# Softmax of a feed-forward attention block: sixteen ScalarE exponentials with bias and row sums, in place of one exponential between three VectorE passes

## The reference, cut to what matters

```
gate_v = x Ws                      top 2 of 8 experts per head, sigmoid weights -> mix_v
v      = mix_v . (x Wv)            [B, 16 heads, 56, 64]
scores = (q * scale) k^T           [B, 16 heads, 56, 56]
probs  = softmax(scores)
attn   = probs v
gate_o = x Wd                      top 2 of 8 experts per head -> mask_o
x      = x + sum over heads of (mask_o attn) Wo
```

## Time and profile before

| what | value |
|---|---|
| median of 3 runs | 551.34 us (551.05 to 553.38) |
| the profiled execution, its own time | 552.02 us |
| its span, first to last instruction | 550.0 us |
| busy share PE / DVE / ACT / POOL | 80% / 85% / 53% / 26% |
| granted TensorE clock, mean | 0.965 |

### The profile page before, as it was taken

The page is one execution under the profiler, slowest core; times in us unless marked ns, Lnnn a source line. Parts: engine busy times, 40 slices in busy tenths (PEclk is TensorE's granted clock), DMA queues, the critical chain, the costliest instruction groups (busy, mean ns, idle before and its releaser), DMA issues.

```text
span 550.0 us, 25189 instructions
## 1 busy us (share of the span) xinstructions
PE 437.6 (80%) x10768; PEld 366.0 (67%) x10768; DVE 468.2 (85%) x850; ACT 293.3 (53%) x400; POOL 143.1 (26%) x125
## 2 busy tenths in 40 slices
PE   1466889889988998658887888788888888887864
PEld 0245777777777877547776776677676767676754
DVE  2987778887888895579999999999999999999962
ACT  1254756766675674425544554555555455545631
POOL 8262767775777685000000000000000000000000
PEclk9987999999999999678999999999999999999996
DMA  7814443454345300000000000000000000000000
GB/s 175 265 40 133 137 155 116 135 182 141 114 161 177 120 1 4 1 1 3 8 3 4 4 4 0 4 4 2 2 4 4 0 4 4 4 0 4 7 7 5
DMA packets 18124, 29.44 MB, mean 54 GB/s; under 512 B 2988, under 2 KB 13996, under 8 KB 18092
## 3 DMA queue, kind: packets, MB, share of 16 engines
q1 hardware_dynamic: 18092, 28.97, 16.9%
HBM read 28.05 MB, written 0.92 MB: 53 GB/s over the span
## 4 chain that ended last, share of the span: by engine, by line
DVE 43%; PE 33%; issue 14%; ACT 6%; DVEq 1%; DMA 1%; SPq 1%; POOL 1%; ACTq 0%; POOLq 0%
DVE ctxf_all L856 8%; PE ps L958 6%; PE ps L1201 5%; DVE ctxf_all L827 5%; DVE rs L844 3%; PE ps L989 3%; DVE ctxT L653 3%; DVE ah L874 2%; DVE attnf L866 2%; ACT ah L557 2%; PE ps L1004 2%; PE ps L1005 2%; PE ps L1006 2%; PE ps L1014 2%; PE ps L1126 1%
## 5 line engine op out<-in xcount | busy, mean ns | idle before, releaser
L369 POOL TENSOR_TENSOR nat<-ctxf_all,nat 128x640 f16<-128x640 f32 x32 | 70.6, 2223 | 50.1 <-ACT nat L442 50.1
L958 PE MATMUL ps<-ident,nat 128*128 128x128 f16 x768 | 60.9, 225 | 10.0 <-DVE ctxT L653 5.2
L442 ACT CAST nat<-ctxf_all 128x1536 f16<-128x1536 f32 x32 | 45.5, 1470 | 39.2 <-PE ps L1006 39.2
L856 DVE TENSOR_TENSOR ctxf_all<-mixp,diag_h 128x3584 f16<-128x3584 f16 x32 | 63.2, 2014 | 0.0
L958 PEld LDWEIGHTS ps<-ident,nat 128*128 128x128 f16 x768 | 46.2, 100 | 23.4 <-issue 13.0
L1098 PE MATMUL ps<-xn,mT 128*128 128x112 f16 x256 | 41.9, 218 | 11.2 <-DVE mixp L851 11.2
L375 POOL TENSOR_TENSOR p<-pf,p 128x672 f16<-128x672 f32 x32 | 46.1, 1460 | 12.8 <-ACT pf L455 12.8
L653 DVE COPY ctxT<-ps 128x1024 f16<-128x1024 f16 x64 | 42.7, 685 | 4.7 <-PE ps L958 4.7
L1201 PE MATMUL ps<-ctxf_all,ah 128*64 128x112 f16 x1024 | 29.6, 219 | 18.5 <-DVE ah L874 18.4
L447 ACT COPY ctxT<-ps 128x1024 f16<-128x1024 f16 x32 | 33.0, 1033 | 20.3 <-PE ps L958 20.3
L973 PE MATMUL ps<-qk_cur,ctxT 128*128 128x56 f16 x384 | 33.5, 188 | 12.6 <-DVE ctxT L653 10.7
(11 more groups left out here) (169 smaller groups left out, 1288.3 us busy)
## 6 DMA issues: line engine op xcount, KB each, us to landing
ctxf_all<-in_ctx_dram SPq DMA_DIRECT2D x32, 704.0 KB
ctxf_all<-in_ctx_dram SPq DMA_DIRECT2D x32, 46.0 KB
x_all<-in_x_dram SPq DMA_DIRECT2D x2, 448.0 KB
out_dram<-y_all SPq DMA_DIRECT2D x32, 28.0 KB
ctxf_all<-in_ctx_dram SPq DMA_DIRECT2D x32, 18.0 KB
fwq_nat<-in_L_ffn_Wq_dram SPq DMA_DIRECT2D x1, 512.0 KB, 9.2
fwk_nat<-in_L_ffn_Wk_dram SPq DMA_DIRECT2D x1, 512.0 KB, 9.6
fwv_nat<-in_L_ffn_Wv_dram SPq DMA_DIRECT2D x1, 256.0 KB, 5.8
```

The lines of the kernel that those rows point to most:

```text
L369: pool.tensor_tensor(nat[k][:, 1, 7 * C:], ctxf[k][:, 7 * C:], nat[k][:, 0, 7 * C:], ALU.subtract).then_inc(natlo2, 1)
L442: act.copy(nat[k][:, 0, :], ctxf[k][:, :]).then_inc(nathi, 1)
L856: last = dve.tensor_tensor(dv[:, part, :, :, :], mixp[:, part, :, :].unsqueeze(2).broadcast_to((P, 2 * NQ, HALF, H)), diag_h[:, :, :].unsq ...
L958: last = pe.transpose(ps[:, (3 * b + c) % 2, :].bitcast(F16)[:, P * (j % 8):P * (j % 8) + P], nat[k][:, j // TK, C * (j % TK):C * (j % TK) ...
```

## The change

The scores' z are evacuated with the factor -SCALE instead of SCALE, so that PSUM holds the scores with their sign turned. DVE takes the row minimum `smn` of those (one 128x896 pass as before), and ACT computes exp(-1 * psum + smn) in 16 instructions of 128x56, each with its column of `smn` as bias and with `accum_out`, which leaves the row's sum in `rs`. The subtraction, its tile `ssub`, and the sum on DVE are gone. The 16 exponentials come in two groups of eight, ahead of `aT` and behind it. On DVE the minimum moves ahead of the low part of `ah`. On ACT `xnT_evac` moves ahead of the high part of `ah`, and `gates_out` from behind the exponential to ahead of it; on PE the gates move from behind the output mix to ahead of it. The evacuation of `vT` covers the same elements in another order: it reads PSUM with a stride of 8 elements and writes runs of 56, where it read runs and wrote with a stride of 128 elements.

```diff
@@ -154,8 +154,7 @@
         dv = ctxf_all[:, 0:n_dv].bitcast(F16).rearrange("p (s k t h) -> p s k t h", s=2, k=NQ * 2, h=H)
         dm = ctxf_all[:, n_dv:n_dv + n_dm].bitcast(F16).rearrange("p (k r t j) -> p k r t j", k=NQ * HG, r=2, j=E // 2)
         pj = ctxf_all[:, n_dv + n_dm:n_dv + n_dm + n_pj].bitcast(F16).rearrange("p (s k d) -> p s k d", s=2, d=DH)
-        smx = sb("smx", [P, 2 * K16])
-        ssub = sb("ssub", [P, 2 * K16, S])
+        smn = sb("smn", [P, 2 * K16])
         e_sb = sb("e_sb", [P, K16, 2, SLOT])
         rs = sb("rs", [P, K16 * 2])
         rinv = sb("rinv", [P, K16 * 2])
@@ -239,9 +238,7 @@
         f_z2e = sem("f_z2e")
         f_s = sem("f_s")
         f_mx = sem("f_mx")
-        f_sub = sem("f_sub")
         f_e = sem("f_e")
-        f_rs = sem("f_rs")
         f_ri = sem("f_ri")
         f_top = sem("f_top")
         f_mo = sem("f_mo")
@@ -518,13 +515,25 @@
                 after(act, f_sg, i)
                 act.activation(th[:, :, :], g_sb[:, 0:16, :], ACT.Tanh, scale=0.5).then_inc(f_th, 1)
+            def exps(i, b):
+
+                if b == 0:
+                    after(act, f_mx, i + 1)
+                    after(act, f_et, i)
+                    after(act, f_ri, i)
+                for k in range(K16):
+                    last = act.activation(e_sb[:, k, b, 0:S], ps[:, b, S * k:S * k + S], ACT.Exp,
+                                          bias=smn[:, K16 * b + k:K16 * b + k + 1], scale=-1.0,
+                                          accum_out=rs[:, 2 * k + b:2 * k + b + 1])
+                last.then_inc(f_e, 1)
+
             def iteration(i, front=True, back=True, nxt=True):
                 if back:
                     after(act, f_vt, i)
                     after(act, f_vv, i - 1)
-                    act.mul(vT[:, :, :, 0:S].rearrange("p h b t -> p b t h"),
-                            ps[:, 6:8, 0:8 * S].rearrange("p b (t h) -> p b t h", h=8), 1.0 / (MIX_UP * PJ_UP)).then_inc(f_vte, 1)
+                    act.mul(vT[:, :, :, 0:S], ps[:, 6:8, 0:8 * S].rearrange("p b (t h) -> p h b t", h=8),
+                            1.0 / (MIX_UP * PJ_UP)).then_inc(f_vte, 1)
                 if front:
                     after(act, f_pj, i + 1)
@@ -533,7 +542,7 @@
                     act.copy(pj[:, 0, :, :], ps[:, 3, :].rearrange("p (q d) -> p q d", d=DH)).then_inc(f_pje, 1)
                     after(act, f_z1, i + 1)
                     after(act, f_s, i)
-                    act.mul(z[:, 0:8, :].rearrange("p (a k) n -> p a (k n)", a=2), ps[:, 0:2, 0:8 * S], SCALE).then_inc(f_z1e, 1)
+                    act.mul(z[:, 0:8, :].rearrange("p (a k) n -> p a (k n)", a=2), ps[:, 0:2, 0:8 * S], -SCALE).then_inc(f_z1e, 1)
                     after(act, f_tr, i + 1)
                     after(act, f_d, i)
@@ -547,7 +556,9 @@
                     after(act, f_z2, i + 1)
                     after(act, f_s, i)
-                    act.mul(z[:, 8:16, :].rearrange("p (a k) n -> p a (k n)", a=2), ps[:, 2:4, 0:8 * S], SCALE).then_inc(f_z2e, 1)
+                    act.mul(z[:, 8:16, :].rearrange("p (a k) n -> p a (k n)", a=2), ps[:, 2:4, 0:8 * S], -SCALE).then_inc(f_z2e, 1)
+                if nxt:
+                    xnT_evac(i + 1)
                 if back:
                     after(act, f_a, i - 1)
@@ -556,7 +567,9 @@
                         after(act, f_nrm, 2 * i - 1 + b)
                         act.copy(ah[:, k, 0, :], attnf[:, k, :]).then_inc(f_ahi, 1)
                 if nxt:
-                    xnT_evac(i + 1)
+                    gates_out(i + 1)
+                if front:
+                    exps(i, 0)
                 if back:
                     after(act, f_a, i)
@@ -564,14 +577,7 @@
                     act.copy(aT[:, :, :, 0:S],
                              ps[:, 4, 0:8 * S].rearrange("p (b t j) -> p j b t", b=2, j=E // 2)).then_inc(f_ae, 1)
                 if front:
-
-                    after(act, f_sub, i + 1)
-                    after(act, f_et, i)
-                    after(act, f_rs, i)
-                    act.activation(e_sb[:, :, :, 0:S].rearrange("p k b j -> p b k j"),
-                                   ssub[:, :, :].rearrange("p (b k) j -> p b k j", b=2), ACT.Exp).then_inc(f_e, 1)
-                if nxt:
-                    gates_out(i + 1)
+                    exps(i, 1)
                 if front:
                     after(act, f_et, i + 1)
@@ -840,9 +846,7 @@
                     normalise(i + 1)
                 if back:
-                    after(dve, f_e, i)
-                    dve.tensor_reduce(rs[:, :], e_sb[:, :, :, 0:S].rearrange("p k b j -> p (k b) j"), AX.X, ALU.add).then_inc(f_rs, 1)
-                    dve.wait_ge(f_rs, i)
+                    after(dve, f_e, 2 * i)
                     dve.reciprocal(rinv[:, :], rs[:, :]).then_inc(f_ri, 1)
                 if front:
@@ -866,22 +870,19 @@
                         dve.tensor_tensor(attnf[:, k, :], ps[:, 6 + b, :].rearrange("p (k d) -> p k d", d=DH),
                                           rinv[:, :].rearrange("p (k b) -> p b k", b=2)[:, b, :].unsqueeze(2).broadcast_to((P, K16, DH)),
                                           ALU.mult).then_inc(f_nrm, 1)
+                if front:
+
+                    after(dve, f_s, i + 1)
+                    after(dve, f_e, 2 * i)
+                    dve.tensor_reduce(smn[:, :], ps[:, 0:2, 0:8 * S].rearrange("p b (k j) -> p b k j", j=S), AX.X, ALU.min).then_inc(f_mx, 1)
+                if back:
+
                     after(dve, f_a, i - 1)
                     for b in range(2):
                         k = slice(K16 * b, K16 * b + K16)
                         dve.wait_ge(f_nrm, 2 * i - 1 + b)
                         dve.wait_ge(f_ahi, 2 * i - 1 + b)
                         dve.tensor_tensor(ah[:, k, 1, :], attnf[:, k, :], ah[:, k, 0, :], ALU.subtract).then_inc(f_alo, 1)
-                if front:
-
-                    after(dve, f_s, i + 1)
-                    dve.tensor_reduce(smx[:, :], ps[:, 0:2, 0:8 * S].rearrange("p b (k j) -> p b k j", j=S), AX.X, ALU.max).then_inc(f_mx, 1)
-                    dve.wait_ge(f_mx, i + 1)
-                    after(dve, f_e, i)
-                    dve.tensor_tensor(ssub[:, :, :].rearrange("p (b k) j -> p b k j", b=2),
-                                      ps[:, 0:2, 0:8 * S].rearrange("p b (k j) -> p b k j", j=S),
-                                      smx[:, :].rearrange("p (b k) -> p b k", b=2).unsqueeze(3).broadcast_to((P, 2, K16, S)),
-                                      ALU.subtract).then_inc(f_sub, 1)
                 if nxt:
                     low_tokens(i + 1)
                 if front:
@@ -1188,6 +1189,7 @@
                     last.then_inc(f_s, 1)
                 if nxt:
                     xn_turn(i + 1)
+                    gates(i + 1)
                 if back:
                     after(pe, f_dm, i)
@@ -1202,8 +1204,6 @@
                                                      dm[:, n, r, :, :].rearrange("p t j -> p (t j)"),
                                                      start=(hg + a == 0), stop=(hg == HG - 1 and a == 1))
                     last.then_inc(f_a, 1)
-                if nxt:
-                    gates(i + 1)
                 if back:
                     after(pe, f_ae, i)
                     if front:
@@ -1214,8 +1214,7 @@
                     last.then_inc(f_o, 1)
                 if front:
-                    after(pe, f_e, i + 1)
-                    after(pe, f_sub, i + 1)
+                    after(pe, f_e, 2 * i + 2)
                     for k in range(K16):
                         last = pe.transpose(ps[:, k // 4, P * (k % 4):P * (k % 4) + P],
                                             e_sb[:, k, :, :].rearrange("p b j -> p (b j)"), ident[:, :])
```

## The result

The changed kernel takes 582.67 us (581.16 to 584.71, 4 runs) against 551.23: a ratio of 1.0562, 95% interval 1.0540 to 1.0584. It is slower by 31.4 us. The forecast was 568, the range 542 to 597.

A forecast was written before the change was run, and what follows sets the result against it. Bound: a closed ring through PE's queue and the softmax on ACT, beyond whose slack DVE's relief wins nothing. 13.2 us over 15 iterations, +3.6 first, -0.5 last: +16.3 on 552.02, less 0.7, gives 568 us; range 542 to 597.

The forecast's parts named there:

- my sum: Whole kernel: 13.2 us for 15 iterations, +3.6 for the first, -0.5 for the last front, together +16.3 us.
- a read that doesn't overlap: Rival on ACT: the sum's read waits for its exponential's end, 0.406 us per exponential, 594 us; chance 0.26.
- the clock: Rival on PE: TensorE clock drops to 0.82 in the loop, +39 us more, 607 us; chance 0.03.
- The ring: Pair loop, PE's queue through scores, softmax and turn: 19.61 us per iteration against 18.73, +0.88 us.
- The softmax part: From the scores' end to the next exponentials' turn: 5.13 us before, 7.71 after; beyond 6.8 the closed loop bounds.
- Iteration 0: First iteration, without a back: 6.9 us where maximum, subtraction and exponential took 3.2, so +3.6 us.
- The price of an exponential: ACT, 56 columns with pointer bias: 0.20 us plus 0.106 for a separate overlapping sum read, 0.306; break-even 0.242.
- free sums: Rival on ACT: accum_out costs nothing, 0.20 us per exponential, 17.95 us per iteration, 542 us; chance 0.18.
- the gates' way ahead of the exponentials: ACT: xnT, ah, gates' copy and tanh delay the exponentials to 2.24 us after the scores; minimum ready at 1.43.
- vT: ACT's copy: 1.81 us before, 0.92 taken for the new order; off the path, worth nothing either way.
- PE's three waits for DVE: PE ahead of projection (0.31), for mixing weights (0.63), for low mix (0.69): 1.63 us per iteration, expected to go.
- The faster rival: Sums come free if an exponential keeps ACT under 0.24 us: 542 us; chance 0.18.

The follow-up runs named there:

- e1: Changed kernel plus 8 extra matmuls of 448 columns per iteration in PE's waits for aT and the exponentials, results unused: 565.64 us, ratio 1.0262.
- e3: Changed kernel without accum_out, the row sums again one 128x896 pass on DVE: 554.48 us, ratio 1.0049.
- e2: Changed kernel with PE's gates, xnT copies and gates' copy with tanh back where the kernel before had them: 560.42 us, ratio 1.0163.
- e5: Changed kernel plus 8 extra matmuls per iteration in PE's waits, vT copy written as before (runs read, stride written): 568.53 us, ratio 1.0309.
- e8: Kernel before with the new vT copy alone: 550.28 us, ratio 0.9968, 12 runs.
- e7: Changed kernel with the old order of gates and xnT, no accum_out, row sums as a tree of additions on GpSimd: 562.58 us, ratio 1.0177.
- e9: Changed kernel with only the gates' copy and tanh moved back behind the last exponential: 571.34 us, ratio 1.0339.
- e4: Kernel before with its own softmax and only the new order on all three engines and the new vT copy: 578.25 us, ratio 1.0488.

## Why the prediction was right or wrong

The change is slower, as forecast, by 31.4 us instead of 17. By the spans of the traces e1, the changed kernel with the clock at full, is 12.7 us over the kernel before, where my sum had 16.3; the mechanism of the sum, a ring made longer by the exponentials, is borne out. The clock's 17 us come on top. That 582.67 still lies in the range is luck: the range was stretched to 597 for a read that doesn't overlap, which the traces rule out (0.285 per exponential, not 0.406), and the clock, which did bring the time up, was named as left out of it.

**The ring: right.** The prediction saw in the kernel before that PE's own round of 11.90 us plus the softmax part is a closed ring with 1.63 us to spare, and that DVE's relief is worth nothing once that is used. At full clock the ring is 19.25 us, where I had 19.61. The softmax part, from the scores' end (429.27) to the turn (436.73), is 7.46 for my 7.71, and more than the 6.8 up to which there was slack. Over 15 iterations of 0.53 that is 8 us instead of 13 above the kernel before; e1 has 10.5 for these, as the first two distances grew by more (21.45 and 19.26 for 18.72 and 17.93), which I hadn't foreseen. Iteration 0 was priced at +3.6 and measured +3.2.

**The price of an exponential: size off by 7%.** The sum's read is a separate instruction, and it overlaps: 0.19 + 0.095 = 0.285 for my 0.306. That is worth 256 x 0.021 = 5 us, my sum would have been 563, and e1, the changed kernel at full clock, measured 565.6. The end of "free sums" at 0.20 was the right price without the read (e3: 0.19). The estimate by the figures of the Trainium skill ("ScalarE: Activation LUTs", What ACT_TABLE_LOAD costs) was 0.234 for it; e3's row has 0.19, so its fixed cost is too long for this form, which reads PSUM.

**The step that failed: the clock.** It was a rival with a chance of 0.03, set aside because "holes of 1.16 us stand in the loop already without any drop". The new kernel has three of about that length in a row, 0.91, 1.21 and 1.16, and the mean clock is below 1.00 in nine of the 15 distances. That cost 17 us, and filling two of the holes won it back (e1). It is more than the ring cost. Nor was its form right: I priced a steady 0.82, +39 us; in the trace it is whole at most times and halved now and then, 0.93 on average from 300 to 520 us. Mean busy share would not have told it either: PE is busy 82 of 100 us in the changed kernel and in e2, with a clock of 0.93 in one and 1.00 in the other.

**The order.** I counted the gates' way ahead of the exponentials into the ring at its right size: from 1.43 to 2.24 after the scores (measured 1.42 and 2.26). What I didn't draw from it is that it makes 0.42 of the 0.53 us by which the iteration is longer, and with the clock 22 us of 31 (e2). Early gates serve DVE's choice of experts, and DVE isn't pressed any more: in e1 it waits 0.93 us per iteration for ACT's projection copy with the mixing weights long done.

**What was hidden stayed hidden.** vT (e5, e8: steady iterations equal to 0.01 us), the sign (the second copy of z takes 0.92 us in both kernels), the minimum (1.08 us). PE's three waits for DVE went, as said: ahead of z the changed kernel's page has 0.8 us of them left in the whole run, where one iteration had 0.69.

**The faster rival** needed under 0.24 per exponential. The chip has a separate read, so the case didn't come. e3 shows the spacing without it, 0.19, and with DVE's sum put back is at 554.5, no gain. Whether the sums, were they free, would give 542 stays open, since e7, meant to show it, was spoiled by GpSimd.

What stays open: which pattern of holes lets the clock fall. e2's 1.77 and 1.2 don't, the changed kernel's 0.3, 0.91, 1.21 and 1.16 do, and so do e9's 0.3, 0.8, 0.7 and 1.2. Nor was it tried whether filling PE in e9 or e4 brings them to their full-clock iterations.

## What to carry to other kernels

Before work is moved off the busiest engine, add up the closed ring that runs through the queue of the second busiest, waits left out; the slack between the two sums is all that a relief can win, and once it is used up every microsecond put on the ring's other engines is paid in full. Here it was 1.6 us, and the sixteen small instructions with a read each cost 3.6 more than the one they replaced. And list the holes that a plan makes in TensorE's queue. Neither the longest of them nor the mean busy share told here whether the clock would fall, so let TensorE do harmless work in them before judging the plan.

## What the hardware showed unexpectedly

- ACT's exponentials of 128x56 with pointer bias start 0.19 us apart (e3); the accumulator read adds 0.09, while the rows have means of 0.34 and 0.25. The exponentials' rows grow from 0.29 to 0.34 within the first eight and to 0.40 within the second, with the distance unchanged.
- A strided write to SBUF in 128x896 took 1.8 us, a strided read of PSUM with a write in runs of 56 took 0.92, no more than the copy of z of that size, which reads and writes in order.
- Additions on GpSimd slowed DVE's half-precision and single-precision passes with two SBUF operands by up to 2.5 times (0.42 to 1.07) while they overlapped; reductions beside them kept 0.42.
